# Attention with positions: all low parts of the rotated terms on GpSimd, and the small operations of two normalizations, but for the powers, on VectorE

## The reference, cut to what matters

```python
def _forward(src, ...):
    x = _layernorm(src, ln1_g, ln1_b)
    q, k, v = ...                              # 16 heads of 8
    ac = jnp.einsum('bihd,bjhd->bhij', q, k)
    bd_full = jnp.einsum('bihd,phd->bhip', q, p)       # p: projected sines and cosines
    bd = bd_full[:, :, jnp.arange(Ss)[:, None], rel]
    att = jax.nn.softmax((ac + bd) * scale, axis=-1)
    attn_out = jnp.einsum('bhij,bjhd->bihd', att, v).reshape(Bs, Ss, Ds) @ wo
    src = src + attn_out
    x2 = _layernorm(src, ln2_g, ln2_b)
    sel = jax.nn.sigmoid(x2 @ sel_w)           # 4 of 32 experts, then the mixture
```

## Time and profile before

| | |
|---|---|
| median of 3 runs | 2753.81 us (2750.35 to 2755.32) |
| the profiled execution's own time | 2752.55 us |
| its span in the trace | 2750.7 us |
| busy: PE, DVE, ACT, POOL | 91%, 72%, 59%, 60% |
| the two attentions of this kind | from about 824 to 1410 us and from about 1933 to 2519 us of the span |

### The profile page before, as it was taken

The page is one execution under the profiler, slowest core; times in us unless marked ns, Lnnn a source line. Parts: engine busy times, 40 slices in busy tenths (PEclk is TensorE's granted clock), DMA queues, the critical chain, the costliest instruction groups (busy, mean ns, idle before and its releaser), DMA issues. The chain is left out here.

```text
span 2750.7 us, 60628 instructions
## 1 busy us (share of the span) xinstructions
PE 2495.7 (91%) x19804; PEld 1914.8 (70%) x19804; DVE 1983.9 (72%) x4717; ACT 1617.5 (59%) x4705; POOL 1659.5 (60%) x2469
## 2 busy tenths in 40 slices
PE   7999799699979999999988988998899999998898
PEld 5788677478868877777777445665787777776843
DVE  4554388455448999999964566775799999996545
ACT  3332254333328988888842335777798888885232
POOL 4322676332317788888843764553668888885376
PEclk9999899899989999999999998999999999999999
DMA  3710366460012222222335136553222222242622
GB/s 121 315 74 1 79 144 140 137 270 1 1 33 47 49 61 62 62 61 52 111 89 168 51 76 138 108 109 77 47 48 61 62 56 53 54 124 62 185 63 67
DMA packets 231991, 241.99 MB, mean 88 GB/s; under 512 B 27538, under 2 KB 203922, under 8 KB 224498
## 3 DMA queue, kind: packets, MB, share of 16 engines
q1 hardware_dynamic: 182530, 196.14, 27.3%
q0 software_dynamic: 12288, 25.19, 3.4%
q10 hardware_dynamic: 36864, 16.79, 2.1%
HBM read 99.28 MB, written 134.41 MB: 85 GB/s over the span
## 5 line engine op out<-in xcount | busy, mean ns | idle before, releaser
L2804 ACT ACTIVATE f4a_pr<-f4a_sr,f4a_nm 128x256 f32<-128x256 f32 x512 | 239.0, 479 | 41.6 <-DVE f4a_nm L2872 40.5
L2804 ACT ACTIVATE f6a_pr<-f6a_sr,f6a_nm 128x256 f32<-128x256 f32 x512 | 238.9, 478 | 41.2 <-DVE f6a_nm L2872 40.1
L3007 POOL TENSOR_TENSOR f4a_rr<-a5b_room 128x256 f32<-128x256 f32 x256 | 196.6, 768 | 86.8 <-DVE a5b_room L2880 82.6
L3007 POOL TENSOR_TENSOR f6a_rr<-a5b_room 128x256 f32<-128x256 f32 x256 | 196.4, 767 | 79.1 <-DVE a5b_room L2880 73.7
L2007 DVE TENSOR_REDUCE a_nm<-a_sr 128x2 f32<-128x512 f32 x256 | 167.0, 685 | 70.2 <-PE a_sr L1739 69.3
L2679 PE MATMUL f4a_sr<-f4a_pe_hi,f4a_rr_hi 128*128 128x256 f32 x512 | 187.6, 366 | 0.0
L2679 PE MATMUL f6a_sr<-f6l_pe_hi,f6a_rr_hi 128*128 128x256 f32 x512 | 187.6, 366 | 0.0
L2880 DVE TENSOR_TENSOR a5b_room<-f4a_ur,f4a_turn 128x512 f32<-128x512 f32 x256 | 172.8, 675 | 19.9 <-PE f4a_ur L2664 18.2
L2872 DVE TENSOR_REDUCE f4a_nm<-f4a_sr 128x2 f32<-128x512 f32 x256 | 174.5, 682 | 14.2 <-PE f4a_sr L2681 13.3
L2872 DVE TENSOR_REDUCE f6a_nm<-f6a_sr 128x2 f32<-128x512 f32 x256 | 174.5, 682 | 14.1 <-PE f6a_sr L2681 13.2
L2880 DVE TENSOR_TENSOR a5b_room<-f6a_ur,f6l_turn 128x512 f32<-128x512 f32 x256 | 172.9, 676 | 15.9 <-PE f6a_ur L2664 13.1
(11 more groups left out here) (631 smaller groups left out, 8259.8 us busy)
## 6 DMA issues: line engine op xcount, KB each, us to landing
slots<-f_zero SPq DMA_DIRECT2D x100, 512.0 KB, 6.1
f4m_xr<-slots SPq DMA_DIRECT2D x128, 64.0 KB, 2.2
slots<-f4m_y ACTq DMA_DIRECT2D x128, 64.0 KB, 2.2
f6m_xr<-slots SPq DMA_DIRECT2D x128, 64.0 KB, 2.2
slots<-f6m_y ACTq DMA_DIRECT2D x128, 64.0 KB, 2.2
r_scratch<-r_parts SPq DMA_DIRECT2D x32, 192.0 KB, 2.3
all_qs<-r_scratch SPq DMA_DIRECT2D x16, 384.0 KB, 4.8
all_ks<-r_scratch SPq DMA_DIRECT2D x16, 384.0 KB, 6.6
```

The source lines that it names most:

```text
L2804: last = nc.scalar.activation(pr[:, n % 4, x, :], sr.bank(b, n)[:, x * T:(x + 1) * T], ACT.Exp, bias=nm[:, n % SB, x:x + 1], accum_out=zs[ ...
L3007: nc.gpsimd.tensor_tensor(rr[:, hs % RAW, :], tmp[:, hs % 2, 0, :], tmp[:, hs % 2, 1, :], ALU.add)\
```

## The change

All sixteen low parts of a sequence are taken by GpSimd, so the VectorE function `rest_of_fourth`, its semaphore and the waits for it are gone. `root` keeps only the power on GpSimd. Two new functions go to VectorE in both classes: `variances` behind the measurement in the same round (two operations in `Lead`, one in `Opening`), and `shift`, one operation, two rounds later (n = 5 in `Lead`, n = 9 in `Opening`, there ahead of the addition to the stream). ScalarE's `normal_twice` moves from n = 5 to n = 6. The same functions serve the plain attention, which prepares the first two sequences of block 6, and the mixture, which normalizes the last sequence.

```diff
+    def variances(self, dve, i):            # Lead
+        dve.wait_ge(self.ln_aggr, i + 1)
+        if i:
+            dve.wait_ge(self.ln_rstd, i)
+        nc.vector.tensor_scalar(self.veps[:, 0, :], self.mv[:, :, 1], EPS, None, ALU.add).then_inc(self.ln_veps, 1)
+        nc.vector.tensor_scalar(self.veps[:, 1, :], self.mv[:, :, 1], 1.0 + EPS, EPS * EPS, ALU.mult, ALU.add).then_inc(self.ln_veps, 1)
     def root(self, pool, i):
-        pool.wait_ge(self.ln_aggr, i + 1)
+        pool.wait_ge(self.ln_veps, 2 * i + 2)
...
+            pool.wait_ge(self.ln_shift, i)
+        self.nc.gpsimd.tensor_tensor(self.rstd..., self.veps..., self.k.minus_half[:, 0:2 * TT], ALU.pow).then_inc(self.ln_rstd, 1)
+
+    def shift(self, dve, i):
+        dve.wait_ge(self.ln_rstd, i + 1)
...
+        self.nc.vector.scalar_tensor_tensor(self.nb[:, :, :], self.mv[:, :, 0].unsqueeze(1).to_broadcast([P, 2, TT]), -1.0,
+                                            self.rstd[:, :, :], ALU.mult, ALU.mult).then_inc(self.ln_shift, 1)
...
         def lows(eng, b, hs):
-            eng.wait_ge(rr_lo_ready, b[0] * (H - H // 4) + hs + 1 - (hs + 3) // 4)
-            if b[0] or hs >= 1:
-                eng.wait_ge(rr_lo_fourth, b[0] * (H // 4) + (hs + 3) // 4)
+            eng.wait_ge(rr_lo_ready, b[0] * H + hs + 1)
...
-                if n == AT["ln"] + 2 and b:
+                if n == AT["ln"] + 3 and b:
                     lead.normal_twice(act, b[0])
...
                         last.then_inc(s1_aggr, 1)
+                        opening.variances(dve, i)
                     if n == 9:
+                        if kept(e):
+                            opening.shift(dve, i)
...
                         lead.measure_tokens(dve, b[0])
+                        lead.variances(dve, b[0])
...
+                    if n == AT["ln"] + 2:
+                        lead.shift(dve, b[0])
...
-            def rest_of_fourth(it, n):
-                b, hs = relating(it, n, AHEAD - 2)
-                if b is not None and hs % 4 == 1:
-                    dve.wait_ge(rr_hi_ready, b[0] * H + hs + 1)
-                    nc.vector.tensor_tensor(rr_lo[:, hs % RRS, :], rr[:, hs % RAW, :], rr_hi[:, hs % RRS, :], ALU.subtract)\
-                        .then_inc(rr_lo_fourth, 1)
...
                 b, hs = relating(it, n, AHEAD - 2)
-                if b is not None and hs % 4 != 1:
+                if b is not None:
                     rest_of_terms(b, hs)
```

More of the change, by code:

```diff
@@ L2041, in small @@
                     lead.measure_tokens(dve, i)
+                    lead.variances(dve, i)
+                i = ahead(s, n, -2)
+                if i is not None:
+                    lead.shift(dve, i)
                 i = ahead(s, n, 15)
@@ L2211, in measure_tokens @@
         if i:
-            dve.wait_ge(self.ln_minus, i)
+            dve.wait_ge(self.ln_shift, i)
         for t in range(TT):
@@ L2226, in root @@
             pool.wait_ge(self.xn_ready, i * TT)
[L2227 to L2237 removed]
+            pool.wait_ge(self.ln_shift, i)
+        self.nc.gpsimd.tensor_tensor(self.rstd[:, :, :].rearrange("p u t -> p (u t)"), self.veps[:, :, :].rearrange("p u t -> p (u t)"),
+                                     self.k.minus_half[:, 0:2 * TT], ALU.pow).then_inc(self.ln_rstd, 1)
+    def shift(self, dve, i):
+        dve.wait_ge(self.ln_rstd, i + 1)
+        if i:
+            dve.wait_ge(self.src_ready, i * TT)
+            dve.wait_ge(self.xn_ready, i * TT)
+        self.nc.vector.scalar_tensor_tensor(self.nb[:, :, :], self.mv[:, :, 0].unsqueeze(1).to_broadcast([P, 2, TT]), -1.0,
+                                            self.rstd[:, :, :], ALU.mult, ALU.mult).then_inc(self.ln_shift, 1)
     def normal_tokens(self, act, i):
@@ L2334, in __init__ @@
         self.spare = a.sb("spare", [P, 2])
-        (self.s1_stats, self.s1_aggr, self.s1_veps, self.s1_rstd, self.s1_minus, self.s1_shift, self.x2_ready, self.gate_step,
+        (self.s1_stats, self.s1_aggr, self.s1_veps, self.s1_rstd, self.s1_shift, self.x2_ready, self.gate_step,
          self.mask_ready, self.counted, self.sums_ready, self.place_step, self.row_ready, self.table_step, self.table_turn,
          self.table_ready, self.fetched, self.gates_ready) = [a.sem(n) for n in (
-             "s1_stats s1_aggr s1_veps s1_rstd s1_minus s1_shift x2_ready gate_step mask_ready counted sums_ready place_step row_ready "
+             "s1_stats s1_aggr s1_veps s1_rstd s1_shift x2_ready gate_step mask_ready counted sums_ready place_step row_ready "
              "table_step table_turn table_ready fetched gates_ready").split()]
@@ L2345, in fetch, with variances, shift @@
             sp.dma_start(self.kv[:, n, :, :], self.io[name]).then_inc(self.fetched, 16)
+    def variances(self, dve, i):
+        dve.wait_ge(self.s1_aggr, i + 1)
+        if i:
+            dve.wait_ge(self.s1_rstd, i)
+        self.nc.vector.tensor_scalar(self.veps[:, :], self.mv[:, :, 1], EPS, None, ALU.add).then_inc(self.s1_veps, 1)
     def root(self, pool, i):
-        nc, k = self.nc, self.k
-        pool.wait_ge(self.s1_aggr, i + 1)
+        pool.wait_ge(self.s1_veps, i + 1)
         if i:
             pool.wait_ge(self.x2_ready, i * TT)
-        nc.gpsimd.tensor_tensor(self.veps[:, :], self.mv[:, :, 1], k.eps[:, 0:TT], ALU.add).then_inc(self.s1_veps, 1)
-        pool.wait_ge(self.s1_veps, i + 1)
-        nc.gpsimd.tensor_tensor(self.rstd[:, :], self.veps[:, :], k.minus_half[:, 0:TT], ALU.pow).then_inc(self.s1_rstd, 1)
-        pool.wait_ge(self.s1_rstd, i + 1)
-        nc.gpsimd.tensor_tensor(self.veps[:, :], self.mv[:, :, 0], self.rstd[:, :], ALU.mult).then_inc(self.s1_minus, 1)
-        pool.wait_ge(self.s1_minus, i + 1)
-        nc.gpsimd.tensor_tensor(self.nb[:, :], self.veps[:, :], k.minus_one[:, 0:TT], ALU.mult).then_inc(self.s1_shift, 1)
+            pool.wait_ge(self.s1_shift, i)
+        self.nc.gpsimd.tensor_tensor(self.rstd[:, :], self.veps[:, :], self.k.minus_half[:, 0:TT], ALU.pow).then_inc(self.s1_rstd, 1)
+    def shift(self, dve, i):
+        dve.wait_ge(self.s1_rstd, i + 1)
+        if i:
+            dve.wait_ge(self.x2_ready, i * TT)
+        self.nc.vector.scalar_tensor_tensor(self.nb[:, :], self.mv[:, :, 0], -1.0, self.rstd[:, :], ALU.mult, ALU.mult)\
+            .then_inc(self.s1_shift, 1)
     def normal(self, act, i):
@@ L2581, in relative_attention @@
         ur = Ring(a.ps("ur", [P, 2, 512]), a.sem("ur_filled"), a.sem("ur_emptied"), H, 2)
-        nm_ready, av_done, rz_ready, rz8_ready, yn_ready, rr_ready, rr_hi_ready, rr_lo_ready, rr_lo_fourth = [a.sem(n) for n in (
-            "nm_ready av_done rz_ready rz8_ready yn_ready rr_ready rr_hi_ready rr_lo_ready rr_lo_fourth").split()]
+        nm_ready, av_done, rz_ready, rz8_ready, yn_ready, rr_ready, rr_hi_ready, rr_lo_ready = [a.sem(n) for n in (
+            "nm_ready av_done rz_ready rz8_ready yn_ready rr_ready rr_hi_ready rr_lo_ready").split()]
         s1_stats, s1_aggr, s1_shift, x2_ready = opening.s1_stats, opening.s1_aggr, opening.s1_shift, opening.x2_ready
@@ L2996, in _ @@
             dve.wait_ge(k.loaded, k.loaded_count)
-            run(step, lambda it, n: (rotated(it, n), rest_of_fourth(it, n)))
+            run(step, rotated)
         @block.gpsimd
@@ L3359, in residual @@
                                                x_t[:, first:first + GROUP, :], ALU.mult, ALU.add).then_inc(finished, 1)
+            opening.shift(dve, LATE)
             for r in range(ROUNDS + 2):
```

19 lines of the change are left out of this document (3 added, 16 removed).

## The result

The changed kernel takes 2834.76 us in the median of four runs (2829.17 to 2835.96), the kernel before 2754.31 us (2750.35 to 2755.32): 1.0291 times, 95% interval 1.0273 to 1.0309. It is 80 us slower. I had forecast 27 us faster; even the upper end of my range, 2757, is 78 us too low.

What follows compares the result with a forecast made beforehand. GpSimd was taken to pace rounds 2 to 10 and late VectorE the rest; -1.35 us per full iteration, ten a stage, two stages, gave -27 us: 2725.5 profiled, 2727 forecast as median, range 2708 to 2757 (forecast's own 2713 to 2735).

Steps and rivals of the forecast that it cites:

- ScalarE waits in round 9: Second normalization, full iterations: ScalarE newly waits 1.9 us for VectorE's product, with round 9's exponentials queued behind.
- it is 0.2 to 0.9 us later: Scores of round 11 on TensorE: delayed by this much through ScalarE's new wait in round 9.
- the freed hold-up: Round 10: VectorE's low part of 2.21 us, which delays the next exponentials, goes and offsets ScalarE's new wait.
- Rounds 14 to 5: Full iterations: the 1.58 us hold-up and two smaller ones go from VectorE, so TensorE gains 1.3 us.
- rival (a): GpSimd's density holds up VectorE's operations with SBUF inputs more often, eating the gain; 2742 to 2756 us, chance 0.18.
- VectorE gains five small operations: In `variances` and `shift`: 0.5 to 0.8 us, plus one to two hold-ups of 0.7 to 1.4 us.
- small operations on VectorE that take over 0.7 us in the median: One of two named signs, on VectorE's new operations, that would make the prediction wrong.
- GpSimd gains four low parts: Full iterations: 2.8 us more on GpSimd, less shorter roots, net +1.1 us, making 34.9 us a floor for the period.
- Rounds 2 to 10: The stretch that GpSimd paces: two low parts come in, both root savings go out, net -0.26 us.
- In the other iterations ... 0: Non-full iterations, paced by TensorE: about 0.6 us from the shorter root cancels against the round-9 wait, net 0.
- rival (b): The 1.9 us round-9 wait reaches TensorE whole: full iterations +0.3 us, the ten others +1 each; 2769 us, chance 0.15.
- The rule on hold-ups: VectorE against GpSimd on SBUF: back-to-back GpSimd operations hold VectorE up longer than one instruction's 0.69 us.

Runs made afterwards that it cites:

- lows_only: The kernel before with all low parts on GpSimd and the small operations still on GpSimd; 2767.53 us, 1.0059 times the kernel before.
- half_before: The kernel before with only the low parts of rounds 10 and 14 (terms 13 and 1) moved to GpSimd; 2747.80 us, 0.9998 times the kernel before.
- normal10: The changed kernel with ScalarE's second normalization moved to round 10, the product staying in round 9; 2751.91 us, 1.0005 times the kernel before.
- half10: The changed kernel with ScalarE's second normalization in round 10 and the low parts of rounds 2 and 6 on VectorE; 2749.79 us, 0.9999 times the kernel before.
- small10: The changed kernel with every fourth low part back on VectorE and ScalarE's second normalization in round 10; 2727.51 us, 0.9920 times the kernel before.
- before_late: The kernel before with ScalarE's second normalization also waiting for VectorE's addition to the stream in round 9; 2771.70 us, 1.0074 times the kernel before.
- before_later: The kernel before with ScalarE's second normalization waiting for VectorE's round-9 addition and the rotation of round 10; 2789.25 us, 1.0132 times the kernel before.

## Why the prediction was wrong, point by point

**"ScalarE waits in round 9": the mechanism was right, the size and what it does were not.** I predicted a new wait of 1.9 us with the exponentials of round 9 and the scores of round 11 behind it; that is what the timeline shows. It is 2.67 us, because I put the product where the addition stands in the kernel before and priced it at 0.12 us, and didn't count that it and the operations ahead of it can be held up. The mask was held up before already; the sums weren't:

```profile
2204.21 0.70 DVE L2476 TENSOR_TENSOR f6o_mask<-f6o_mask 128x32 bf16<-128x32 bf16 x1
2204.94 0.18 DVE L2478 TENSOR_TENSOR f6o_sums<-f6o_sums,f6o_mask 128x32 bf16<-128x32 bf16 x1
```

In the changed kernel the mask takes 0.58 us, the sums 0.70 and the product 0.39, around GpSimd's addition and low part of 2217.94 and 2218.63. From the start of round 9's maxima to that of the product it is 2.18 us, where it was 1.77 to the addition. From round 10 to round 11 the scores are 2.71 us later and not "0.2 to 0.9"; that is beyond the 1.5 us that I had named as the sign of being wrong.

**The step that failed: the scores of round 11, "it is 0.2 to 0.9 us later", and with them "Against this stands the VectorE hold-up of 2.21 us in round 10, which delays the next exponentials today and is gone", so that "by round 13 TensorE stands between 0.4 us earlier and 0.3 us later".** Measured, TensorE is 23.98 - 21.59 = 2.39 us later at round 13, and 3.66 where the clock falls. Of the two sides of the cancellation the freed hold-up was priced about right: from 0.2 to 0.9 down to -0.4 to 0.3 is 0.6 us, and `lows_only` and `half_before`, where the hold-up is gone and nothing else stands in front, gain 0.7 (4.54 us from round 11 to 13 in place of 5.24). The side that failed is the wait: at the scores of round 11 it is not 0.2 to 0.9 us but 2.7 (10 to 11: 5.19 us in place of 2.48). Two things make the difference. The wait itself is 0.8 us longer, 2.67 in place of 2205.5 - 2203.64 = 1.86. And I had let ScalarE's readiness (2203.64) and the scores of round 10 (2204.97) stay 1.3 us apart as in the earlier trace rows, so that most of the wait would be absorbed; in the changed kernel they are 0.1 us apart (2216.75, which is 2219.42 - 2.67, and 2216.85). The scores of round 10, which GpSimd's low part held back before, now follow ScalarE's exponentials of round 8. So 0.6 + 0.8 + 1.2 = 2.6 of the 2.7 us are accounted for.

**"Rounds 14 to 5", -1.3 us, was wrong.** From round 13 to the next round 4 the changed kernel takes 14.9 us in place of 15.24, `lows_only` 15.18, and `half_before`, which takes away just the two hold-ups on which I had built the term, 15.2 to 16.1. I had taken the 2.1 us that TensorE waits outside GpSimd's half as if all of it could go. Other VectorE operations are held up in their place. Two lines of the changed kernel (minimum, median, maximum ns), the one-hot product of the counting and the last operation of the parts:

```profile
L2499 DVE TENSOR_TENSOR f6o_one<-f6o_one,f6o_place x24: 496/826/1627, 2092.2 to 2524.9; 128x128 f32<-128x128 f32 x24
L2311 DVE TENSOR_TENSOR f6l_parts<-f6l_rest,f6l_parts x15: 679/1914/1923, 1981.2 to 2513.6; 128x512 bf16<-128x512 f32 x15
```

and the same two of the kernel before:

```profile
L2482 DVE TENSOR_TENSOR f6o_one<-f6o_one,f6o_place x24: 273/278/826, 2052.4 to 2456.0; 128x128 f32<-128x128 f32 x24
L2301 DVE TENSOR_TENSOR f6l_parts<-f6l_rest,f6l_parts x15: 733/885/935, 1940.9 to 2444.6; 128x512 bf16<-128x512 f32 x15
```

In eight full iterations the one-hot products take 14.8 us in place of 8.2, the last operation of the parts 15.3 in place of 7.1: 0.8 and 1.0 us an iteration. That is how VectorE lost four low parts, worth 39.6/8 = 4.95 us there (my four terms add up to 4.94; with the 0.54 of waiting that is 5.5 and not the 5.3 that I wrote), and was busy only 0.3 us less an iteration, not the 2 to 4 I wrote. So far this is my rival (a): `normal10`, without the long wait, came out at 2751.9 us, inside its 2742 to 2756. But the number is partly luck, since these hold-ups don't price it: `half10` has the one-hot products back at 280 ns in the median and is only 0.06% below `normal10`. What costs in `normal10` by the table is GpSimd's own way to the scores of round 10.

**"VectorE gains five small operations", 0.5 to 0.8 us and one to two hold-ups of 0.7 to 1.4: right in size.** In block 6 of the changed kernel the medians of `Lead`'s two are 321 and 766 ns, of `Opening`'s 385, of the products 93 and 392; together 1.96 us. That "small operations on VectorE that take over 0.7 us in the median" would make the prediction wrong was a bad sign: they do so in `small10` too, the fastest kernel (705 ns for `Lead`'s first, 775 for `Opening`'s).

**"GpSimd gains four low parts", net +1.1 us: about right** (31.6 to 32.4 us an iteration), but its floor of 34.9 wasn't reached, since it waited for VectorE. "Rounds 2 to 10", -0.26: measured +0.1 to +0.25 at round 10 with the late product in the way, and -0.4 in `normal10` without it. The two terms behind it were each right in sign and about right in size, -1.35 for 0.94 + 0.70 and +1.0 to 1.6 for two low parts of 0.69.

**"In the other iterations ... 0" was wrong.** Early ones take 0.1 and 0.6 us more, the third 36.96 in place of 34.7, and the last two about 39 to 40 and 27.9 to 29.5 in place of 35.2 and 25.0, with a fallen clock in some; 22 us in all. `before_late` and `before_later` show that it is these that pay for a late ScalarE even where the full ones don't: in stage 6 +1.1 to 1.9 us each of the first two, +3.5 to 4.5 each of the last two. I had priced this at 1 us in rival (b) and at nothing in the forecast.

**The rivals.** (b), whose wait "decides once more than about 1.7 us of the wait reach the scores", is what happened, and 2.71 us did. The chance of 0.15 was far too small, and its 2769 us are 66 too low. Over the twenty full periods it kept the -1.3 of a step that doesn't exist (measured -0.3, 20 us) and had the wait at 1.9 instead of 2.7 us (16 us); the clock, about 16 us, was in none of my cases, and the rest is in the ten other iterations, 22 us in place of 10. What I had for it, "two score buffers only" and a ScalarE without a gap in rounds 9 to 12, weighed more than the freed hold-up that I set against it: I named it there with its 2.21 us of VectorE, and it is worth 0.7 us of TensorE.

**The rule on hold-ups.** The one-hot product of the changed kernel takes up to 1627 ns against 273 at best in the kernel before, 1.35 us of waiting, which is two starts of GpSimd at 0.69 and not one; so the longer hold-ups that I went by are real. By the wording of the Trainium skill (SBUF — State Buffer, "Who interferes with whom"), that who issues first gets the shared pair for the whole instruction, such a wait would end with that one instruction. The trace disagrees where GpSimd's operations follow each other without a gap.

**What stays open.** Whether the kernel before would gain by its normalization in round 10. Why the clock falls behind some of these waits and not behind others: TensorE had been busy 1.47 of the 4 us before the waits' end in the iteration that kept it and 1.48 of 4 in the one that lost it. And why the low parts of terms 1 and 13 are free to move in the kernel before and cost 0.8% in `small10`: `half10` is 0.24 us behind it at round 10 and at round 13 still, and loses up to another 1 us in the rounds to the next round 4, which I haven't followed.

## What to carry to other kernels

A small operation that goes to another engine takes that engine's place in line with it: look at what its consumer's queue holds behind the wait, and move the consumer with it. Here one round later for ScalarE's normalization was worth 2.9% in the changed kernel, more than all else in the change. And price a hold-up by what its consumer starts late, not by its own length: 2.21 us of VectorE were worth 0.7 us of TensorE, while 1.6 us of small operations ahead of GpSimd's critical work were worth 1.35.
